# Masks of the nodes moved to DRAM, deeper rings in the attention pipeline, and a later transposition of the weighted rows

## What is computed

```python
logits = (x @ wr).reshape(B, N, H, 4).transpose(0, 2, 1, 3)     # 16 heads, 4 nodes
tk_vals, tk_idx = jax.lax.top_k(logits, 2)
member = jax.nn.one_hot(tk_idx, 4).sum(axis=-2) > 0
pos = jnp.cumsum(member, axis=2) - member
for n in range(4):
    qr, kr = rotate(q, pos[..., n]), rotate(k, pos[..., n])
    scores = jnp.where(causal & member[..., n][:, :, None, :], qr @ kr.T * D ** -0.5, NEG)
    outs.append(softmax(scores) @ v)
y = (softmax(tk_vals)[..., None] * take(outs, tk_idx)).sum(axis=3)
```

## Time and profile before

| | |
|---|---|
| median of 3 runs | 1045.87 us (1040.52 to 1046.56) |
| profiled execution, its own time | 1042.09 us |
| span of the profiled execution | 1040.3 us |
| PE busy in the span | 880.0 us (85%) |
| DVE, ACT, POOL busy | 776.9, 748.7, 617.7 us |

### The profile page before, as it was taken

One profiled execution on the slowest core, in us unless ns is written; L12 is line 12 of the kernel. 1 busy time (PEld: TensorE's weight loads), 2 busy tenths in 40 slices (PEclk: granted clock), 3 DMA queues, 4 the chain that ended last, 5 costly groups with the idle time before them and its releaser, 6 DMA issues.

```text
span 1040.3 us, 18878 instructions
## 1 busy us (share of the span) xinstructions
PE 880.0 (85%) x5651; PEld 608.0 (58%) x5651; DVE 776.9 (75%) x1840; ACT 748.7 (72%) x2024; POOL 617.7 (59%) x869
## 2 busy tenths in 40 slices
PE   4338989999998998999899989999999996867883
PEld 3326656666666666656666657666676655534552
DVE  6999969957987797789778867996776755445443
ACT  6327787888888888877987888878887885333441
POOL 3157757857886786778677866886665630240222
PEclk9669989999999999999999999999999997789996
DMA  9000001001000000010000000010000041020003
GB/s 217 5 1 7 12 16 28 23 12 33 22 22 23 22 22 22 23 32 23 20 24 22 23 22 22 26 29 8 3 3 2 3 182 61 13 86 1 19 24 97
DMA packets 45602, 32.66 MB, mean 31 GB/s; under 512 B 8032, under 2 KB 43488, under 8 KB 45504
## 3 DMA queue, kind: packets, MB, share of 16 engines
q1 hardware_dynamic: 44288, 28.95, 9.7%
q0 software_dynamic: 1216, 2.51, 0.7%
HBM read 18.30 MB, written 12.36 MB: 29 GB/s over the span
## 4 chain that ended last, share of the span: by engine, by line
PE 63%; DVE 23%; ACT 6%; issue 5%; another core or an unknown queue 1%; POOL 1%; DMA 0%; ACTq 0%; DVEq 0%; POOLq 0%; SPq 0%
PE psum L1126 21%; PE psum L1148 7%; PE psum L1233 6%; PE psum L1140 6%; PE psum L1067 5%; PE psum L1111 4%; DVE pcs L805 3%; PE psum L1131 3%; DVE arena L753 3%; ACT probs L549 3%; DVE accs L861 2%; PE psum L1169 2%; DVE psum L850 2%; PE psum L1113 2%; PE psum L1128 2%
## 5 line engine op out<-in xcount | busy, mean ns | idle before, releaser
L1126 PE MATMUL psum<-QK 128*128 128x128 f32 (+3 forms) x1024 | 372.9, 449 | 4.9 <-ACT QK L528 4.9
L549 ACT ACTIVATE probs<-psum,negmax 128x128 f32<-128x128 f32 (+3 forms) x512 | 267.3, 530 | 108.3 <-DVE negmax L850 75.1
L390 POOL TENSOR_TENSOR R<-pcs 128x512 f32<-128x512 f32 x128 | 207.2, 1639 | 64.1 <-DVE pcs L805 46.8
L850 DVE CUSTOM_DVE_ANT_0 psum<-psum,causal 128x384 f32<-128x384 f32 (+1 forms) x256 | 156.9, 636 | 75.5 <-PE psum L1131 75.3
L1126 PEld LDWEIGHTS psum<-QK 128*128 128x128 f32 x1024 | 164.8, 193 | 49.3 <-issue 41.2
L416 POOL TENSOR_TENSOR coef<-rden,wslot 128x2 f32<-128x2 f32 x256 | 68.3, 267 | 177.2 <-DVE rden L856 177.1
L805 DVE TENSOR_TENSOR pcs<-psum,arena 128x512 f32<-128x512 f32 x256 | 161.6, 672 | 0.0
L861 DVE SCALAR_TENSOR_TENSOR accs<-probs,coef,accs 128x128 f32<-128x128 f32 (+3 forms) x256 | 157.6, 616 | 1.0 <-ACT accs L558 1.0
L558 ACT ACTIVATE accs<-probs,coef 128x128 f32<-128x128 f32 (+3 forms) x256 | 148.6, 581 | 11.5 <-POOL coef L416 10.7
L1140 PE MATMUL psum<-ident,accs 128*128 128x128 f32 x640 | 116.3, 280 | 46.5 <-ACT QK L528 41.9
L528 ACT ACTIVATE QK<-psum 128x384 f32<-128x384 f32 x256 | 126.7, 495 | 0.9 <-PE psum L1113 0.7
(11 more groups left out here) (211 smaller groups left out, 1473.3 us busy)
## 6 DMA issues: line engine op xcount, KB each, us to landing
weight_halves<-whl SPq DMA_DIRECT2D x48, 128.0 KB, 2.2
arena<-weight_halves SPq DMA_DIRECT2D x7, 768.0 KB, 7.1
wst<-in_L_ffn_w_up_dram SPq DMA_DIRECT2D x14, 128.0 KB, 2.6
wst<-in_L_ffn_w_gate_dram SPq DMA_DIRECT2D x14, 128.0 KB, 2.5
wst<-in_L_ffn_w_down_dram SPq DMA_DIRECT2D x14, 128.0 KB, 2.5
sorted_rows<-arena SPq DMA_DIRECT2D x1, 1430.0 KB, 12.1
QK<-sorted_rows SPq DMA_DIRECT2D x5, 260.0 KB, 4.0
x<-in_L_attn_x_dram SPq DMA_DIRECT2D x4, 256.0 KB, 4.1
```

The costliest lines, as they stand in the source:

```text
L390: pool.tensor_tensor(R[u][:, :, :, 0:3:2, half * HALF:(half + 1) * HALF].rearrange("p t e j f -> p (t e) j f"), halves(pc, half), halves(p ...
L549: act.activation((expB if e else expA)[:, k % (4 if e else 3), 0:w], area, ACT.Exp, scale=1.0 if k % TB < 2 else -1.0, bias=negmax[k % 4][ ...
L850: dve.tensor_tensor_reduce(score_area(k, e), score_area(k, e), causal[:, T - w:T], -1.0, 3e38, ALU.add, ALU.min, accum_out=negmax[k % 4][: ...
L1126: pe.matmul(o, QK[:, u, e, rows], QK[:, u, 2, 0:w], start=True, stop=False)
```

## The change

- `prob_rows`, and ACT's `move_pt` with it, handle a step one later: at step k PE transposes the rows of step k - 5 and ACT moves those of k - 6. The list `turns` is changed alike, so pt(k-5) now stands behind t(k+2).
- The ring of slot 0's exponentials goes from 3 to 4, of slot 1's from 4 to 5, that of `acc` from 4 to 6, and the waits that guard them move by as much.
- `mk` loses its buffer. ACT writes the masks into three parts of `accT` that are free at that time, SP writes them to a DRAM tensor with three DMAs, waits for them, and fills `mring` from there.
- `xsT` now lies in `accs`, where `h2T` lies too, so ACT waits for `h2_low` (the last reader of `h2T`) before it writes `xsT`.

```diff
+RACC = 6
-        mk = sb("mk", [P, B, 3, T], F16)
+        mk_d = nc.dram_tensor("node_rows", [HD, B, 3, T], F16, kind="Internal").ap()
-        probs = sb("probs", [P, 7, T])
-        expA, expB = probs[:, 0:3, :], probs[:, 3:7, :]
+        probs = sb("probs", [P, 9, T])
+        expA, expB = probs[:, 0:4, :], probs[:, 4:9, :]
-        accs = sb("accs", [P, 4, T])
-        acc = [accs[:, g, :] for g in range(4)]
+        accs = sb("accs", [P, RACC, T])
+        acc = [accs[:, g, :] for g in range(RACC)]
...
+        mk = [accT_flat[:, a:a + 1024].bitcast(F16).rearrange("p (b t) -> p b t", b=B) for a in (2560, 4096, 5120)]
...
-        xsT = mk[:, :, :, :].rearrange("p b k t -> p (b k t)")[:, 0:2 * SORTED * P].rearrange("p (l t) -> p l t", l=2)
+        xsT = accs_flat.bitcast(F16)[:, 0:2 * SORTED * P].rearrange("p (l t) -> p l t", l=2)
...
-            if 0 <= k - 4 < STEPS:
-                turns.append(("pt", k - 4))
+            if 0 <= k - 5 < STEPS:
+                turns.append(("pt", k - 5))
...
-            sp.wait_ge(S["mk_ev"], 6)
+            for kind in range(3):
+                sp.wait_ge(S["mk_ev"], 2 * kind + 2)
+                sp.dma_start(mk_d[:, :, kind, :], mk[kind][0:HD, :, :]).then_inc(S["mk_out"], 16)
+            sp.wait_ge(S["mk_out"], 48)
...
-                sp.dma_start(mring[0:NODES, r, :, :], mk[h * NODES:(h + 1) * NODES, b, :, :]).then_inc(S[f"mm_in{r}"], 16)
+                sp.dma_start(mring[0:NODES, r, :, :], mk_d[h * NODES:(h + 1) * NODES, b, :, :]).then_inc(S[f"mm_in{r}"], 16)
...
-                if k >= 3:
-                    act.wait_ge(S["wa_done"], k - 2)
                 if k >= 4:
-                    act.wait_ge(S["acc_done"], k - 3)
+                    act.wait_ge(S["wa_done"], k - 3)
+                if k >= 5:
+                    act.wait_ge(S["acc_done"], k - 4)
...
-                if k >= 4:
-                    act.wait_ge(S["pt_done"], k - 3)
+                if k >= RACC:
+                    act.wait_ge(S["pt_done"], k - RACC + 1)
...
-                if 0 <= k - 5 < STEPS:
-                    move_pt(k - 5)
+                if 0 <= k - 6 < STEPS:
+                    move_pt(k - 6)
...
+            act.wait_ge(S["h2_low"], B)
...
-                if 0 <= k - 4 < STEPS:
-                    prob_rows(k - 4)
+                if 0 <= k - 5 < STEPS:
+                    prob_rows(k - 5)
```

More of the change, by code:

```diff
@@ L171, in block_kernel @@
         gcol4 = R[1][:, :, :, :, :].rearrange("p t e j d -> p (t e j d)")[:, 0:B * P].rearrange("p (b d) -> p b d", b=B)
-        h2T = accs[:, :, :].rearrange("p g t -> p (g t)")
+        accs_flat = accs[:, :, :].rearrange("p g t -> p (g t)")
+        h2T = accs_flat[:, 0:TOKENS]
         hrows = yT_flat[:, 0:NT * ROW].rearrange("p (t c) -> p t c", c=ROW)
         xrows = QK_flat[:, 0:SORTED * ROW].rearrange("p (t c) -> p t c", c=ROW)
-        xsT = mk[:, :, :, :].rearrange("p b k t -> p (b k t)")[:, 0:2 * SORTED * P].rearrange("p (l t) -> p l t", l=2)
+        xsT = accs_flat.bitcast(F16)[:, 0:2 * SORTED * P].rearrange("p (l t) -> p l t", l=2)
         probs_flat = probs[:, :, :].rearrange("p g t -> p (g t)")
@@ L506, in _ @@
                 act.wait_ge(S["mk_t"], i + 1)
-                act.activation(mk[0:HD, half * 2:half * 2 + 2, kind, :],
+                act.activation(mk[kind][0:HD, half * 2:half * 2 + 2, :],
                                bank16[(0, 1, 2, 3, 6, 0)[i]][0:HD, :].rearrange("p (b t) -> p b t", b=2), ACT.Copy,
@@ L548, in exponentials @@
                     act.wait_ge(S["negmax_done"], 2 * k + e + 1)
-                    act.activation((expB if e else expA)[:, k % (4 if e else 3), 0:w], area, ACT.Exp,
+                    act.activation((expB if e else expA)[:, k % (5 if e else 4), 0:w], area, ACT.Exp,
                                    scale=1.0 if k % TB < 2 else -1.0, bias=negmax[k % 4][:, e:e + 1], accum_out=den[k % 4][:, e:e + 1]
@@ L554, in weigh_a @@
                 w = (k % TB + 1) * P
-                if k >= 4:
-                    act.wait_ge(S["pt_done"], k - 3)
+                if k >= RACC:
+                    act.wait_ge(S["pt_done"], k - RACC + 1)
                 act.wait_ge(S["coef_done"], k + 1)
-                act.activation(acc[k % 4][:, 0:w], expA[:, k % 3, 0:w], ACT.Copy, scale=coef[k % 4][:, 0:1]
+                act.activation(acc[k % RACC][:, 0:w], expA[:, k % 4, 0:w], ACT.Copy, scale=coef[k % 4][:, 0:1]
                                ).then_inc(S["wa_done"], 1)
@@ L860, in weigh_b @@
                 dve.wait_ge(S["wa_done"], k + 1)
-                dve.scalar_tensor_tensor(acc[k % 4][:, 0:w], expB[:, k % 4, 0:w], coef[k % 4][:, 1:2], acc[k % 4][:, 0:w],
+                dve.scalar_tensor_tensor(acc[k % RACC][:, 0:w], expB[:, k % 5, 0:w], coef[k % 4][:, 1:2], acc[k % RACC][:, 0:w],
                                          ALU.mult, ALU.add).then_inc(S["acc_done"], 1)
@@ L1139, in prob_rows @@
                 for jb in range(ib + 1):
-                    mm_ = pe.transpose(psPT[:, jb * P:(jb + 1) * P], acc[k % 4][:, jb * P:(jb + 1) * P], ident[:, :])
+                    mm_ = pe.transpose(psPT[:, jb * P:(jb + 1) * P], acc[k % RACC][:, jb * P:(jb + 1) * P], ident[:, :])
                 mm_.then_inc(S["pt_done"], 1)
```

2 lines of the change are left out of this document (1 added, 1 removed).

## The result

The changed kernel takes 1053.2 us (median; 1041.0 to 1057.4), the kernel before 1045.4 us beside it on the same chip (1039.7 to 1047.9). The ratio is 1.0071, with the interval 1.0049 to 1.0092. So it is 0.7% slower: within 1%, as forecast, but +7.8 us where the sum said +1.0, and the median lies 0.2 us past the high end of the range. The profiled execution took 1047.95 us, its span 1046.2.

What follows compares the result with a forecast made beforehand. The prediction took the attention to be bound by PE's own matmuls, leaving 6.9 us idle in 100. Terms of +0.8 and +0.2 us gave +1.0 on 1045.87, so 1046.9 us, range 1037 to 1053.

Steps and rivals of the forecast that it cites:

- the sum: Whole kernel: +0.8 us for moved transposes and +0.2 us for the drain, +1.0 us together; all other parts 0.
- the wait for the PSUM bank: Before `prob_rows` on PE: the wait for `keep_qk` ends last and isn't relaxed, so about 40 us of stalls stay.
- the relaxed data wait: `prob_rows`' wait for `acc_done`, eased by a step of DVE; not the one that ends last: 0 us.
- The first rival: The `acc_done` wait before `prob_rows` is the real one: 28.9 us go, 1017 us; chance 0.10 with its weak form.
- the weight loads' wait for L861 goes from the list: Sign in the list of waits: the 28.9 us put down to `weigh_b` disappear while the stalls stay.
- the room: Masks over DRAM (0, bounds 0 to +3 us) and deeper rings of exponentials and `acc` (0 us) change nothing.
- The second and fourth rival: Second: deeper rings remove all stalls before `prob_rows`, 1004 us, chance 0.02. Fourth: late mask loads delay each head, 0.01.
- the moved transposes: `prob_rows`' transposes change place around the long stalls: +0.11 us a round, +0.8 us in total, bounds -4 to +4.
- the short waits at s = 1 and s = 2: ACT's wider move at s = 1, less PE cover at s = 2: 0 together, bounds -2 to +7 us.
- The third rival: Four transposes at s = 0 delay the scores of s = 1, 0.33 us a head: 1067 us; chance 0.08.
- Work in front of a long stall is free, since the stall ends when ACT's chain does: PE's transposes in the attention: only those behind a long stall count, about 0.11 us each.

Runs made afterwards that it cites:

- after: The changed kernel itself, first run, against the kernel before: 1053.2 us, ratio 1.0071.
- masks_rings: Kernel before with the masks moved over DRAM and the deeper rings, `prob_rows` still at k - 4: 1044.5 us, ratio 1.001.
- after_again: The changed kernel run once more, unedited, against the kernel before: 1049.0 us, ratio 1.006.
- masks_late: Changed kernel with the old rings of exponentials (3 and 4), later `prob_rows` and masks over DRAM kept; against the kernel before: 1050.8 us, ratio 1.006.
- masks_only: Kernel before with only the masks moved over DRAM, old rings in use and `prob_rows` at k - 4: 1043.5 us, ratio 1.000.
- before_stretched: Kernel before with one tiny ACT instruction ahead of `keep_qk` at s = 3 of every eighth head: 1042.0 us, ratio 1.009.
- late_filled: Changed kernel with three redundant transposes more at s = 3 in two heads of each eight; against the kernel before: 1026.3 us, ratio 0.994.
- late_filled_again: Changed kernel with the same three redundant transposes, repeated on a third chip; against the kernel before: 1027.1 us, ratio 0.996.
- before_project: Kernel before with `project(n+3)` moved ahead of `prob_rows` at s = 3: 1032.3 us, ratio 1.001.
- late_project: Changed kernel with `project(n+3)` moved ahead of `prob_rows` at s = 3; against the kernel before: 1039.9 us, ratio 1.009.
- before_filled: Kernel before with three redundant transposes more at s = 3 in two heads of each eight: 1028.5 us, ratio 0.997.
- late_filled_more: Changed kernel with six redundant transposes at s = 3 in two heads of each eight, fifteen in head 5; against the kernel before: 1025.1 us, ratio 0.994.

## Why the prediction was right and wrong

**Right: which wait is real.** The forecast that the wait for the PSUM bank ends last, that the relaxed data wait gives nothing, and that the stalls stay (1.4 to 2.1 us, 43.8 us in total) held. The first rival (1017 us) fell. The proof needs no estimate: in the timeline of after, the weight loads at 262.17 are put down to L869, at 260.71; but the later `prob_rows` no longer reads what that instruction writes, it reads the step before. So the name in that row can't be the releaser.

**Wrong in a detail: "the weight loads' wait for L861 goes from the list".** It stayed, 29.4 us in 17 times (28.9 in 18 before). I expected it to go because the wait itself is relaxed. But as this case shows, the list goes on naming a line from which the instruction no longer takes anything, so neither this row's presence nor its sum says that the wait ends last.

**Right: the room.** Masks over DRAM 0 (measured 1.000), deeper rings 0 (1.001). The second and fourth rival fell. The prediction took two heads for 12 us; they are some 25, which only adds to the cover of the later mask loads. The Trainium skill's rule from "Perfetto Trace Analysis", Identifying Performance Opportunities, was weighed rightly: with more room in SBUF the waits of `prob_rows` for `keep_qk` stay, 41.5 us in `masks_rings` against 41.9.

**Right in place, off in size and sign: the moved transposes.** The sum had +0.11 us a round from them, and the short waits at s = 1 and s = 2 as 0 together. At the full clock a round became 0.6 to 1.0 us shorter. ACT's waits for row maxima at s = 1 fell from 2.18 us a round to 0.70; those at s = 2, which the prediction feared for, rose from 7.13 to 7.62. That the one is what makes the round shorter is argued, not shown by a run. Over seven rounds the gain is some 4.6 us, inside the two bounds together (-4 to +4 for the moved transposes, -2 to +7 for these waits), but on the other side of zero than the value taken. The range added all bounds as -4 and +8; added plainly they give -6 and +15, so its ends were closer than its own terms allow. The third rival (1067 us), whose round would have been longer in every head, fell with it.

**The step that failed: "Work in front of a long stall is free, since the stall ends when ACT's chain does".** It is free as time of PE, but not for what the chip does with the idle time. The later order took one transpose from in front of and one from behind both long waits at s = 3. Where the wait stands behind the angle product it grew from 1.85 us to between 1.92 and 1.94 in 14 of 20 cases. Where it stands behind the sines it even shrank, from 2.04 to 1.94, but a second wait follows it (0.51 us before, 0.62 after at five of the six places), and from the begin of the first to the end of the second there are now 0.52 us of work in 3.08 us, where there were 0.63 in 3.18. The sum had no term for the clock; the earlier trace rows showed 1.00, and I took it as given. The term it lacked is six to eight stretches at some 1.6 us, +10 to +13 us; with -4.6 for the rounds that makes +5 to +8, where the attention took 5.1 us more with six (after), 8.3 with seven (after_again) and 8.7 with eight (masks_late). That the time still stayed within 1% of before is in part luck: two terms that the sum didn't have nearly cancel.

How far this is shown: that the later order alone brings the loss (masks_late), that it goes with the lower clock in every run, that the same order with filled waits loses most of it (three stretches are left) and is faster than before, and that the early order with a wait stretched by 0.1 us has a loss too, with six stretches. Counted over the profiled executions: the waits at s = 3 by what they stand behind, and how many of them had the lower clock begin within 4 us (the first one of a kernel, near 163 us, is left out where its length is another, 1.89 to 2.45 us: 1 of 5 was followed):

| waits, their length | kernels | followed |
|---|---|---|
| sines, 2.03 to 2.04 us | before, masks_only, masks_rings | 2 of 18 |
| sines, 1.94 us | after (three runs), masks_late | 20 of 24 |
| angle product, 1.85 us | before, masks_only, masks_rings | 0 of 17 |
| angle product, 1.83 to 1.85 us | after, after_again | 0 of 6 |
| angle product, 1.92 to 1.94 us | after (three runs), masks_late | 8 of 14 |
| angle product, 1.94 to 1.96 us | before_stretched | 3 of 6 |
| sines, 1.61 us | late_filled, late_filled_again | 4 of 11 |
| angle product, 1.57 to 1.60 us | late_filled, late_filled_again | 0 of 12 |
| sines, 2.03 to 2.04 us | before_stretched, before_project | 3 of 12 |
| sines, 1.94 us | late_project | 4 of 5 |
| sines, 1.71 us | before_filled | 1 of 6 |
| sines, 1.28 to 1.29 us | late_filled_more, one in late_filled | 3 of 7 |
| angle product, 1.26 to 1.28 us | late_filled_more | 0 of 6 |
| angle product, 1.53 us | before_filled | 0 of 5 |
| s = 0, 1.86 to 1.88 us | late_project | 3 of 6 |

So the length of a wait doesn't decide alone (first two rows): behind the sines the later order has the shorter wait and seven times the share that is followed, and taking it down to 1.28 us didn't bring that share under that of the unfilled early order. And the same wait in the same kernel is followed by the lower clock in one round and not in the next. In the kernel before, the wait of 2.04 us at 214.45 was followed, and the five others at the sines, of 2.03 to 2.04 us and with the same work around them, were not. A rival to the length is therefore open: it may count when a wait falls. The later order and the stretched wait change the length of a round, and each stretch that comes or stays away shifts every wait behind it in time; no run shifted the waits and left them as they were. What is shown is that the later order brings the stretches and the stretches the loss; why these waits and not others was not tested and stays open.

## What to carry to other kernels

Where PE is over 90% busy, its idle time still counts in two ways: as time, and by what the clock does behind it. When moving PE work away from beside a wait of 1.5 us or more, look for stretches of lower clock behind it: here waits that came out 0.1 us longer were followed by a loss of some 1.6 us in about half of the cases, though what decides it is open. If such a wait can't be closed, redundant transposes in it cost no time here, and the later order had three stretches with them instead of eight to ten; the loss shows in the count of instructions per window, since the busy share hides it.

## What the hardware showed that was not expected

- Waits of 1.85 us were never followed by the lower clock (0 of 17), waits of 1.93 at the same place in more than half of the cases (8 of 14). Whether the 0.08 us or the moment decided was not separated. Nearly every stretch in the attention lasts 3.4 us, and one cost 1.1 to 1.9 us of a round.
- 5.3 us of added, redundant transposes made the changed kernel 10.8 us faster (1037.9 to 1027.1, medians of one group). The Trainium skill says in "TensorE: Matmul & The Clock Gate", Part 4: PE-mode transpose, of a transpose that "it doesn't count as PE-busy the same way". Here filling with transposes alone took the stretches at 1.2 GHz from ten to three, and fifteen of them in head 5 took away the one that stands there in the 13 other profiled runs, which speaks for their counting in this kernel.
- The single runs of the changed kernel lie between 1041 and 1057 us. Which waits are followed by the lower clock differs from one execution to the next (eight, nine and ten stretches in its three profiled ones), which may be a part of it; the rest was not followed.
- The chips differ: the kernel before took 1045 us on the first and 1032.6 and 1031.8 us on the two others, 1.2%, more than the whole effect studied. The changed kernel's part behind the attention took 171.2 us in the first profile and 160.8 on the third chip, with 59.5 and 49.0 us of it at the lower level. Why was not followed.
